# The down router's input stored token by token instead of feature by feature

## The reference, cut to what matters

```
def kmoe(x_flat, W_router, A, B, scale, bias, ..., top_k):
    logits = x_flat @ W_router.T
    vals, idx = top_k(logits, 2)
    probs = softmax(vals)
    ...                                   # two experts of 64 per token
h = kmoe(x_flat, W_up, A_up, B_up, ...)   # 64 x 64 = 4096 features per token
h = gelu(h, approximate=False)
y = kmoe(h, W_down, A_down, B_down, ...)  # its router: (tokens x 4096) @ (4096 x 64)
```

## Time and profile before

| | us |
|---|---|
| median of 3 runs | 1339.0 (1336.48 to 1341.79) |
| the profiled execution's own time | 1340.02 |
| its span | 1338.2 |
| PE / PEld busy | 1218.3 / 975.4 |
| ACT busy | 1086.6 |
| DVE / POOL busy | 964.2 / 595.4 |
| mean granted clock, as a share of full | 0.96 |

### The profile page before, as it was taken

How to read it: one execution, slowest core, us unless ns; L and a number is a source line. 1 busy time by engine, 2 the same in 40 slices (tenths; PEclk the granted TensorE clock), 3 DMA queues, 4 the chain that set the end, 5 groups by cost and what they waited for, 6 DMA issues and landing times.

```text
span 1338.2 us, 51821 instructions
## 1 busy us (share of the span) xinstructions
PE 1218.3 (91%) x16466; PEld 975.4 (73%) x16466; DVE 964.2 (72%) x3677; ACT 1086.6 (81%) x3158; POOL 595.4 (44%) x1846
## 2 busy tenths in 40 slices
PE   7799899999999999999999999999999999988645
PEld 5567687777778787777778777777878777765534
DVE  1465779696877869696887969597887959686634
ACT  2465899898988989898989989898889979887663
POOL 2122436363544636264544635364554626352432
PEclk9899999999999999999999999999999999998655
DMA  9200101010010101010010101001010101001000
GB/s 290 45 9 18 34 13 42 15 39 22 19 42 10 42 12 42 17 36 25 17 36 17 41 12 41 20 26 34 14 39 13 41 16 36 17 16 28 9 19 10
DMA packets 66209, 42.57 MB, mean 32 GB/s; under 512 B 18065, under 2 KB 64786, under 8 KB 65682
## 3 DMA queue, kind: packets, MB, share of 16 engines
q1 hardware_dynamic: 65938, 39.25, 10.5%
HBM read 34.98 MB, written 4.19 MB: 29 GB/s over the span
## 4 chain that ended last, share of the span: by engine, by line
PE 56%; DVE 16%; issue 10%; SPq 9%; ACT 3%; DMA 2%; POOL 1%; DVEq 1%; POOLq 0%; ACTq 0%
SPq L478 8%; PE P L797 5%; PE P L765 5%; PE PT L820 5%; PE X L855 4%; PE P L776 4%; PE PT L855 4%; PE P L754 3%; PE F L935 3%; PE X L842 3%; DVE own L1121 3%; PE F L960 3%; DVE chosen_dn L418 3%; PE S L813 3%; PE G L894 2%
## 5 line engine op out<-in xcount | busy, mean ns | idle before, releaser
L418 POOL COPY chosen_dn<-experts 64x64 f32 x1000 | 222.5, 279 | 219.2 <-issue 149.8
L657 ACT ACTIVATE probs<-probs,neg_max 128x128 f32<-128x128 f32 (+1 forms) x512 | 226.4, 444 | 23.6 <-DVE neg_max L1080 20.4
L404 POOL COPY chosen_up<-experts 32x128 f32 x512 | 182.8, 357 | 105.2 <-POOL chosen_up L404 51.7
L404 ACT COPY chosen_up<-experts 32x128 f32 x528 | 156.1, 296 | 17.3 <-PE G L941 4.5
L1080 DVE CUSTOM_DVE_ANT_0 probs<-S,distance 128x128 f32<-128x128 f32 (+1 forms) x512 | 151.9, 351 | 14.6 <-PE S L813 11.1
L820 PE MATMUL PT<-ident,probs 128*128 128x128 f32 x768 | 136.7, 287 | 10.6 <-DVE probs L1098 7.8
L696 ACT ACTIVATE hT<-h 64x1024 f32<-64x1024 f32 x64 | 126.7, 1980 | 8.5 <-DVE h L1211 7.1
L1098 DVE TENSOR_TENSOR probs<-probs,rinv 128x768 f32<-128x768 f32 x128 | 129.1, 1009 | 4.4
L765 PE MATMUL P<-ctxT,wk 128*128 128x256 f32 x512 | 122.3, 383 | 0.9 <-DVE x L1058 0.9
L776 PE MATMUL P<-wv,ctxT 128*128 128x256 f32 x512 | 122.5, 382 | 0.0
L820 PEld LDWEIGHTS PT<-ident,probs 128*128 128x128 f32 x768 | 86.4, 142 | 49.1 <-issue 31.5
(11 more groups left out here) (131 smaller groups left out, 2836.2 us busy)
## 6 DMA issues: line engine op xcount, KB each, us to landing
chosen_up<-in_experts_up SPq DMA_DIRECT2D x992, 16.0 KB, 1.6
x<-in_x SPq DMA_DIRECT2D x16, 256.0 KB, 2.6
ctxT<-in_ctxT SPq DMA_DIRECT2D x16, 256.0 KB, 2.8
out<-x2b SPq DMA_DIRECT2D x16, 256.0 KB, 2.2
experts<-in_experts_up SPq DMA_DIRECT2D x2, 1024.0 KB, 19.4
wk<-in_xWk SPq DMA_DIRECT2D x1, 1024.0 KB
wo<-in_xWo SPq DMA_DIRECT2D x1, 1024.0 KB
wv<-in_xWv SPq DMA_DIRECT2D x1, 1024.0 KB, 7.6
```

Source lines behind the costliest of these rows:

```text
L404: last = copy(to[row:row + D1, n * 2 * F1:(n + 1) * 2 * F1], experts_up[k][:, bass.ds(held[g % loaded(units), unit], 2 * F1)])
L418: last = copy(dst, src.rearrange("p (m c) -> p m c", m=2))
L657: act.activation(probs[:, e % 4, lo:hi], probs[:, e % 4, lo:hi], ACT.Exp, bias=neg_max[:, e % 4, rt:rt + 1], scale=-1.0, accum_out=rsum[:, ...
```

## The change

`hT` gets its two free axes exchanged: token outside, slice inside. `gelu`'s four instructions read `h` in runs of 32 neighbouring floats (the next run 64 floats on) and write 1024 neighbouring floats. The weights of each of the 32 matmuls of the down router are then 64 floats that lie 32 floats (128 bytes) apart. No instruction is added or removed, and the order of steps, the semaphores, the sizes and the arithmetic stay.

```diff
-        hT = sb("hT", [P, F1 // 2, TOKENS])
+        hT = sb("hT", [P, TOKENS, F1 // 2])
...
-                        src = h[half * F1:(half + 1) * F1, :].rearrange("p (n h o) -> p h o n", h=2, o=F1 // 2)[:, oh]
-                        dst = hT[oh * F1:(oh + 1) * F1, :, half * TOKENS // 2:(half + 1) * TOKENS // 2]
+                        src = h[half * F1:(half + 1) * F1, :].rearrange("p (n h o) -> p h n o", h=2, o=F1 // 2)[:, oh]
+                        dst = hT[oh * F1:(oh + 1) * F1, half * TOKENS // 2:(half + 1) * TOKENS // 2, :]
                         act.activation(dst, src, ACT.Gelu).then_inc(hT_ready, 1)
...
-                    mm = pe.matmul(G[to:to + F1, 0:EXPERTS], hT[:, o, :], r_dn[:, o, :],
+                    mm = pe.matmul(G[to:to + F1, 0:EXPERTS], hT[:, :, o], r_dn[:, o, :],
                                    start=(o < 2), stop=(o >= F1 // 2 - 2))
```

## The result

The changed kernel takes 1366.6 us (median of 4 runs, 1366.51 to 1367.44) against 1337.7 for the kernel before, measured beside it (4 runs, 1334.72 to 1341.79): ratio 1.022, 95% interval 1.020 to 1.024. Slower by 29 us, where the forecast was 1361.5 with a range of 1333 to 1392.

A forecast was written before the change was run, and what follows sets the result against it. TensorE was taken to bound the steady turns, with gelu on ACT covered. From 1340.0 us: +23.3 (14 turns), +0.3 (batch 14), -3.7 and +2.5 (batch 15) gave 1362.4, as a median 1361.5; range 1333 to 1392.

The forecast's parts named there:

- ScalarE's part: gelu's four hT instructions: 1980 to 1050 ns each, 3.7 us less per batch, worth 0 in a steady turn.
- TensorE's part: Down router's 64 strided weight loads per batch: burst 1.7 us longer, 23.3 us over 14 steady turns.
- batch 14: Router burst near the end: 1.7 us longer less 1.37 us of room, +0.3 us.
- The argument from rates: Router's weight load: TensorE's 0.81 ns per column is near ScalarE's plain rate, so strided columns cost twice plain ones.
- the middle case: Router's burst: a strided column costs twice a plain one, halves side by side, 1.7 us added per batch.
- The lower bound: Router's weight load: nothing added, as VectorE's own takes 412 ns against 409 for a contiguous 256.
- Batch 15: End of the run, without cover: gelu -3.7 us, the router's burst at half clock +2.5 us.
- the two ends named: Last burst at half clock: +3.3 us if the load's penalty doubles, 0 if streaming covers it.
- B: Router's weight load doesn't feel the distance; only the end changes, -3.7 us, 1335.5 us; chance 0.22.
- C: Both column halves' router loads get in each other's way: 4.8 us per turn, 1412 us; chance 0.13.
- D: ACT sets the turn, TensorE's load costs nothing: 55 us off at most, more likely 1310 to 1330; chance 0.06.
- E: Distance in the router's loads costs little, under 1 us per turn: 1337 to 1349 us; chance 0.06.

The follow-up runs named there:

- ScalarE's half alone: The changed kernel's gelu reads and writes kept, but the router loads 64 neighbouring floats as weights: ratio 0.9964 to the kernel before, median 1333.0 us.
- one half alone: The changed kernel with all 32 router slices in the lower column half: 1419.8 us; the same on the layout of before: 1366.2 us (single runs).

## Why the prediction was right, by its own steps

**ScalarE's part.** Held: 1055 ns for 1050, ACT down by 58 us for 59.5, value 0 in a steady turn. The kernel with this half alone shows it (turn 76.27 against 76.19), and so do the three waits after gelu. The reason given, that the read's distance and not the function costs, held too: runs of 2 floats were enough for 1092 ns. `own`, which the prediction called as a witness, is a weak one, since it also writes its neighbours 4 floats apart (`own_parts`); no run takes its read and its write apart.

**TensorE's part.** The mechanism held: nearly no slack in the load, the halves side by side, a strided load of twice the time. The term that was mis-sized is the added time per record, 26 ns forecast and 31 measured (59.8 less 28.8). The forecast's period of 110 ns is what one half alone shows (111); two halves at once take 120, which it left out. In place of 64 x 26 ns the burst grew by about 2.04 us, and the turn by 2.15. Forecast for the 14 steady turns and batch 14: 23.6 us; measured from the first burst to batch 15's gelu: 30.2. These 6.6 us are more than the shortfall of the whole sum, 4.2; the rest was made up by batch 15 (below) and by a start 1.0 us shorter.

Why it doubled was not foreseen, and the close value is in part luck. The argument from rates for taking it (an engine that asks sooner feels the distance more) is not shown, and the forecast added 52 ns of load to a period of 58, whereas the runs fit a load that takes 1.8 ns for each 16 bytes touched and sets the period once this exceeds 58: nothing added at 8 bytes, 88 ns at 12, 116 at 16. With such a price the middle case could have been worked out from ScalarE's row too: 1980/1024 = 1.93 ns per element that lies alone, near the 1.8 here. The lower bound, that VectorE doesn't feel the distance, was read against another operation; contiguous copies are at the end of this document.

The Trainium skill's rule (Advanced Engine Details and Errata, SBUF Cachelines: lines of 16 bytes, two hits on a line needed for full speed) is borne out by the traces: 2 floats apart nothing is added, 4 apart nearly as much as 32 apart. The formula columns / 1.2 ns of the Trainium skill's TensorE: Matmul & The Clock Gate, section LDWEIGHTS (loading the stationary operand), gives 53 ns for 64 columns at any distance; with 128 bytes between them loads followed each other every 111 ns on one half, so here it can hold for neighbouring columns only.

**Batch 15.** gelu -3.5 for -3.7. The burst was given +2.5 and took +0.5 (4.21 for 3.70): the strided load doesn't slow with the clock, which is near the lower of the two ends named. The reason for going nearer to the upper, that plain records double at half clock, was a misreading as well: 3.68 for 2.09 is 1.76 times. About 2 us too much here stand against the 6.6 too little in the turns.

**The rivals.** B (a port that doesn't feel the distance) and C (the loads in turn, 4.8 us per turn) are out by the burst of 4.13 us, D by ScalarE's half alone, E (under 1 us per turn) by turns 2.15 us longer. C had a grain in it: the strided halves cost each other 9 ns per load.

**Sum.** +22.4 forecast from the profiled execution, +26.6 measured between the profiled spans, +28.8 between the medians (the median of before was 1337.7 here, the 1339.0 of the forecast lies within its spread). Of the 13 turns before, one took 78.9 us and not 75 to 77; no term rests on it.

## What to carry to other kernels

Where one engine writes a buffer transposed and another reads it, one of them steps over a distance; give the neighbouring floats to the one on the chain. Here the layout took 58 us off an engine with 8 us of slack a turn and put 31 ns on each of 1024 loads of the one without. And neither had to pay: with blocks of two floats both found two neighbours within 16 bytes, and the kernel was faster than with either pure layout. And read the load's pace in its burst before touching a weight layout: 58 ns of period over 52 of load says that little can be added there unseen.

## What the runs showed of the hardware that was not expected

- TensorE's weight load of 64 columns of 32-bit floats: free at 8 bytes from column to column, 1.5 times the period at 12, twice from 16 on, with 16, 128 and 132 bytes within 5% of each other. Its stream: twice at 128 bytes, the only distance run on it.
- Strided loads of two column halves run side by side, at 120 ns each instead of 111.
- A strided burst that runs partly at half clock is no longer than at full clock (7.32 against 7.31 us on one half), while a plain one at nearly the same mean clock goes from 3.89 to 5.43, and on both halves, wholly at half clock, from 2.09 to 3.68.
- VectorE may pay for the distance after all. The 409 ns that its 412 for `own` were held against the earlier trace rows are of an instruction of another kind, and the trace of the kernel before has a copy of contiguous elements that is quicker:

```profile
L404 DVE COPY chosen_up<-experts 32x128 f32 x16 | 3.9, 243 | 0.4
```

VectorE's one copy that writes 1024 neighbouring elements (line 1000, which spreads a small table) takes 694 ns, so an estimate from these two, (694 - 243)/896 = 0.50 ns per element, gives 307 ns for 256 contiguous ones. `own` takes 105 ns more, with a read 64 floats and a write 4 floats apart; no run changed either.
